# Six of twelve softmax tiles summed by accumulating transfers, four multiplied with the context in three rounded terms

## The chip, the cores and the metric

The kernel runs on one core of one Trainium2 chip. The metric is the device time of one execution in microseconds; the time of the kernel before is the median of three runs. The core has a matrix engine (TensorE, PE in the profile; its weight loads are PEld), a vector engine (VectorE, DVE), an activation engine (ScalarE, ACT), a general engine (GpSimd, POOL), a queue that only issues transfers (SyncE, SP) and 16 DMA engines. Each engine runs its own queue in order, and the queues meet in semaphores. Transfers issued by SP are on the queue that the profile calls q1, those issued by POOL on q0.

## The reference

One layer of cross attention and one of experts, in float32: 8 batches of 56 query tokens against 1500 context tokens, 16 heads of 64, width 128.

```
q, k, v = layernorm(x) @ Wq, ctx @ Wk, ctx @ Wv          # split into 16 heads
dots = q @ k.T / 8  - (1 - mask) * 1e6                   # the mask is of the query row
x = x + (softmax(dots) @ v) @ Wout + bout
h = gelu(layernorm(x) @ w1[e] + b1[e])                   # batch e goes to expert e
out = x + h @ w2[e] + b2[e]
```

## The kernel before, in words

The key weights are folded into the queries and the value weights into the output weights, so that both attention products are taken with the context itself. A batch is a product of scores (context by 16 x 56 = 896 query columns), an exponential, and a product of the exponentials with the context.

The context is cut into 12 **tiles** of 125 rows. A batch is 12 **steps** t = 0 to 11 (`iteration` on each engine). In step t, PE makes the scores of tile t (`scores`, L405): three terms of rounded operands, high times high, high times low, low times high, each in two halves of 448 columns. Such a rounded operand has the type F32R in the code. ACT takes the exponential (`exponentials`, L639) into a ring of six buffers, `ex`, and then copies the row of shifts into the PSUM buffer that the scores of tile t + 2 will be added to (`seed`, L644). PE multiplies the exponentials of tile t - 2 with the context (`probs_ctx`, L433), in plain float32, two halves of 448 columns, accumulating over all 12 tiles in `ps_a`. The products of tiles 10 and 11 fall into steps 0 and 1 of the next batch.

VectorE adds up the exponentials of the 12 tiles (`add_tile`, L807), 11 additions a batch, at places given by `ADD_AT`: tiles 1 and 2 in step 3, then 3, 4 and 5 in steps 5, 7 and 9, the others from step 10 on, and 10 and 11 at the start of the next batch. The sum over the rows is then a small PE product (`sum_jobs`), for which ACT rounds the sum (`sum_high_part`, L655) and VectorE takes the rest (`sum_low_part`, L952).

Beside this, each batch prepares the next one. In 21 max jobs PE makes the scores once more in one rounded term (`max_job`, L450), at the places in `MAX_AT`, and VectorE takes their maxima (`max_part`, L810). They share two PSUM banks, and a job waits until the job two before it has been drained. From the maxima VectorE makes the shifts (`shifts`, L815 to L821), behind the last max job; PE spreads them in step 10 (`shift_jobs`, L419). The last batch has no such jobs. Every second batch from batch 2 on also carries the expert layer of two batches.

POOL loads and rounds the next batch's context (`ctxt_hi_load`, L1104), and takes the low parts of its queries (L1096) and of its context (`ctxt_lo_chunk`, L1114) at steps 2, 3, 6 and 7. SP loads the raw context (`load_ctxt`, L283) once these low parts are made, and the context by rows (`load_ctx`, L289).

The wait that guards a buffer of the ring:

```
wait(act, pv_done, b.at(TM, t - RING + 1))
wait(act, ex_summed, ...)
nc.scalar.activation(half(ex[0:MT, slot, :]), src, ACT.Exp, scale=SCALE).then_inc(ex_ready, 1)
```

Of the kernel before, what the change touches and what calls it, by code (L numbers as in the profile page):

```python
# [32 lines left out]
ALU = mybir.AluOpType  # L33
# [67 lines left out]
def xattn_ffn(nc, x_pairs, ctx, ctx_t, mask_q, wq_t, wk_t, wv_t, w_out, b_out, w1, b1_t, w2, b2, out):  # L101
# [15 lines left out]
    RING = 6  # L117
    assert D == P and MT * TM == M and QT * P == Q and MC * KM == M and E == B and TM % RING == 0
# [23 lines left out]
    ADD_AT = {(3, 0): (1, 2), (5, 1): (3,), (7, 1): (4,), (9, 1): (5,), (10, 0): (6,), (10, 2): (7,), (11, 0): (8, 9)}  # L142
    ADD_LATE = (10, 11)
# [7 lines left out]
    with ExitStack() as stack:  # L151
# [16 lines left out]
        ex = sb("ex", [P, RING, Q])  # L168
# [12 lines left out]
        wqk_raw = ex[:, :, :].rearrange("p r q -> p (r q)")[:, 0:2 * HP * P].rearrange("p (w j d) -> p w j d", w=2, j=HP)  # L181
# [58 lines left out]
        last_half = sem("last_half")  # L240
        ex_summed, pv_done, att_ready = sem("ex_summed"), sem("pv_done"), sem("att_ready")
# [9 lines left out]
        block = stack.enter_context(nc.Block())  # L251

# [20 lines left out]
        def _(sp):  # L273
# [353 lines left out]
        def _(act):  # L627
# [3 lines left out]
            def exponentials(b, t):  # L631

                slot = t % RING
# [3 lines left out]
                wait(act, pv_done, b.at(TM, t - RING + 1))  # L637
                wait(act, ex_summed, b.at(TM - 1, max(t - RING, 1)) if t >= RING else b.at(TM - 1, t - RING + 1))
# [564 lines left out]
```

## Time and profile before

| | |
|---|---|
| median of 3 runs | 386.22 us (385.52 to 386.38) |
| the profiled execution's own time | 386.32 us |
| its span in the trace | 384.6 us |
| TensorE busy | 372.8 us, 97% |
| VectorE busy | 299.6 us, 78% |
| ScalarE busy | 222.6 us, 58% |
| GpSimd busy | 75.8 us, 20% |
| moved by DMA | 25.00 MB |

The span is the time between the first and the last instruction in the trace; the rest of the profiled execution's own time, 1.7 us, lies around it. A busy share is a mean over the whole span, and several engines can be busy at once.

### The profile page before, as it was taken

How to read it: one execution, taken by the hardware profiler on the slowest of the kernel's cores; microseconds unless marked ns; L12 is line 12 of the kernel's file. 1: busy time of each engine (PE TensorE's matmuls, PEld its weight loads, DVE VectorE, ACT ScalarE, POOL GpSimd, SP SyncE). 2: the span in 40 equal slices, each digit the busy share in tenths (PEclk: the TensorE clock that was granted, in tenths of full speed). 3: DMA queues.
4: the chain of work that ended last, by engine and by line, in shares of the span. 5: the costliest groups of instructions: out<-in, count | busy, mean ns of one | idle time of the engine just before them, and what ended most of it. 6: DMA issues, size and time to landing. Idle time of an engine off the chain costs nothing.

```text
span 384.6 us, 5442 instructions
## 1 busy us (share of the span) xinstructions
PE 372.8 (97%) x1661; PEld 268.2 (70%) x1661; DVE 299.6 (78%) x472; ACT 222.6 (58%) x294; POOL 75.8 (20%) x68
## 2 busy tenths in 40 slices
PE   6999999999999999999999999999999999999994
PEld 6767776677767876677767776777667876676663
DVE  4888677987798669987898679987898679466553
ACT  3556354785468346775577446775577355856521
POOL 0703300720073000810081001800090000000000
PEclk9999999999999999999999999999999999999999
DMA  7665020350035000334035000243032000300000
GB/s 246 220 184 145 2 80 1 82 147 13 3 81 142 20 1 1 87 101 167 0 84 153 3 0 18 84 131 123 0 96 64 0 0 2 115 0 2 0 3 5
DMA packets 23686, 25.00 MB, mean 65 GB/s; under 512 B 1240, under 2 KB 20600, under 8 KB 23672
## 3 DMA queue, kind: packets, MB, share of 16 engines
q1 hardware_dynamic: 20648, 19.45, 16.7%
q0 software_dynamic: 3024, 5.38, 5.4%
q8 instruction: 8, 0.13, 0.1%
q14 instruction: 6, 0.05, 0.1%
HBM read 24.59 MB, written 0.23 MB: 65 GB/s over the span
## 4 chain that ended last, share of the span: by engine, by line
PE 76%; DVE 13%; issue 7%; DMA 1%; ACT 1%; DVEq 1%; SPq 0%; ACTq 0%
PE ps_a L433 29%; PE ps_s L405 24%; PE ps_x L450 9%; PE ps_x L483 4%; DVE ex_sum L807 4%; DVE chunk_max L810 2%; PE ps_a L382 2%; PE ps_x L503 2%; PE ps_x L512 1%; DVE shift_diag L821 1%; DMA ex<-in_wk_t 1%; PE ps_x L465 1%; PE ps_x L466 1%; PE ps_x L419 1%; DVE hid L911 1%
## 5 line engine op out<-in xcount | busy, mean ns | idle before, releaser
L433 PE MATMUL ps_a<-ex,ctx_sb 125*128 125x448 f32 x376 | 167.9, 541 | 0.0
L810 DVE TENSOR_REDUCE chunk_max<-ps_x 128x1 f32<-128x500 f32 x168 | 110.9, 675 | 30.0 <-PE ps_x L450 26.8
L639 ACT ACTIVATE ex<-ps_s 125x896 f32<-125x896 f32 x96 | 88.0, 916 | 70.4 <-PE ps_s L405 68.9
L807 DVE TENSOR_TENSOR ex_sum<-ex_sum,ex 125x896 f32<-125x896 f32 x80 | 91.9, 1149 | 6.7 <-ACT ex L639 5.4
L644 ACT COPY ps_s<-shift_row 125x896 f32<-125x896 f32 x94 | 85.6, 911 | 16.8 <-DVE shift_row L947 14.3
L433 PEld LDWEIGHTS ps_a<-ex,ctx_sb 125*128 125x128 f32 x376 | 69.9, 190 | 25.7 <-issue 19.8
L405 PE MATMUL ps_s<-qk_hi,ctxt_hi 128*125 128x448 f32 x192 | 87.1, 535 | 0.0
L450 PE MATMUL ps_x<-ctxt_hi,qk_hi 128*128 128x500 f32 x168 | 84.0, 503 | 1.3 <-DVE chunk_max L810 0.9
L405 PEld LDWEIGHTS ps_s<-qk_hi,ctxt_hi 128*125 128x125 f32 x192 | 36.0, 187 | 35.1 <-issue 35.0
L405 PE MATMUL ps_s<-qk_hi,ctxt_lo 128*125 128x448 f32 x192 | 54.8, 367 | 0.0
L405 PE MATMUL ps_s<-qk_lo,ctxt_hi 128*125 128x448 f32 x192 | 54.6, 366 | 0.0
L1104 POOL DMA_DIRECT2D ctxt_hi<-in_ctx_t x21 | 11.7, 557 | 175.6 <-PE ps_s L405 173.6
L450 PEld LDWEIGHTS ps_x<-ctxt_hi,qk_hi 128*128 128x128 f32 x168 | 31.5, 188 | 18.2 <-DVE chunk_max L810 9.7
L1114 POOL TENSOR_TENSOR ctxt_lo<-ctxt_raw,ctxt_hi 128x500 fp32r<-128x500 f32 x24 | 40.2, 1688 | 9.3 <-DVE ctxt_hi L827 9.3
L405 PEld LDWEIGHTS ps_s<-qk_hi,ctxt_lo 128*125 128x125 f32 x192 | 35.5, 185 | 4.4
L405 PEld LDWEIGHTS ps_s<-qk_lo,ctxt_hi 128*125 128x125 f32 x192 | 35.6, 185 | 3.4
L1096 POOL TENSOR_TENSOR qk_lo<-qk,qk_hi 128x448 fp32r<-128x448 f32 x16 | 22.2, 1389 | 18.1 <-DVE qk_hi L831 17.2
L685 ACT ACTIVATE logv<-veps 128x1 f32<-128x1 f32 (+2 forms) x7 | 1.4, 204 | 24.9 <-DVE veps L893 22.7
L483 PEld LDWEIGHTS ps_x<-w_vo,att_n 128*128 128x128 f32 (+1 forms) x128 | 14.4, 178 | 1.7 <-DVE chunk_max L810 1.1
L838 DVE TENSOR_TENSOR log_sum<-ps_x,inv_sum 128x448 f32<-128x448 f32 x16 | 9.3, 619 | 7.7 <-ACT inv_sum L672 7.7
L483 PE MATMUL ps_x<-w_vo,att_n 128*128 128x128 f32 (+1 forms) x128 | 15.1, 276 | 0.0
L666 ACT ACTIVATE log_sum<-ps_x 128x448 f32<-128x448 f32 x16 | 7.9, 541 | 9.6 <-PE ps_x L466 6.9
(96 smaller groups left out, 264.0 us busy)
## 6 DMA issues: line engine op xcount, KB each, us to landing
ctxt_raw<-in_ctx_t SPq DMA_DIRECT2D x8, 750.0 KB, 7.3
ctx_sb<-in_ctx SPq DMA_DIRECT2D x8, 750.0 KB
ctxt_hi<-in_ctx_t POOLq DMA_DIRECT2D x21, 250.0 KB, 3.5
w_sb<-in_w SPq DMA_DIRECT2D x4, 512.0 KB, 3.8
w_sb<-in_w SPq DMA_DIRECT2D x8, 256.0 KB, 4.3
ex<-in_wq_t SPq DMA_DIRECT2D x2, 256.0 KB, 3.6
ex<-in_wk_t SPq DMA_DIRECT2D x2, 256.0 KB, 4.5
att_n<-in_wv_t SPq DMA_DIRECT2D x1, 512.0 KB, 6.0
```

Of the source, the lines that this page charges most:

```text
L405: mm = nc.tensor.matmul(dst[c], a[:, u, rows], q[:, u, chunks[c]], start=(n == 0 and not seed), stop=(n == 2 and seed), skip_group_check=seed)
L433: mm = nc.tensor.matmul(ps_a[:, c, 0:CH], ctx_sb[0:MT, u, t, :], ex[0:MT, t % RING, c * CH:(c + 1) * CH], start=(t == 0), stop=(t == TM - 1))
L450: nc.tensor.matmul(bank[:, 0:MC], qk_hi[:, u, t * P:(t + 1) * P], ctxt_hi[:, u, k * MC:(k + 1) * MC], start=True, stop=True).then_inc(job_ ...
L483: mm = nc.tensor.matmul(bank[pair.tokens(), 0:D], att_n[:, h, pair.tokens()], w_vo[:, h, :], start=(h == 0), stop=(h == HEADS - 1))
L639: nc.scalar.activation(half(ex[0:MT, slot, :]), src, ACT.Exp, scale=SCALE).then_inc(ex_ready, 1)
L644: nc.scalar.copy(ps_s[0:MT, t % 2, :, 0:CH], half(shift_row[0:MT, b.parity, :])).then_inc(seeded, 1)
L807: nc.vector.tensor_tensor(dst, left, ex[0:MT, t % RING, :], ALU.add).then_inc(ex_summed, 1)
L810: nc.vector.tensor_reduce(chunk_max[:, k, t:t + 1], filled()[:, 0:MC], AX.X, ALU.max).then_inc(job_free, 1)
L838: nc.vector.tensor_tensor(log_sum[:, cols], bank[:, 0:CH], inv_sum[:, cols], ALU.mult).then_inc(job_free, 1)
L1096: nc.gpsimd.tensor_tensor(qk_lo[:, b.parity, cols], b.pick(qk)[:, cols], qk_hi[:, b.parity, cols].bitcast(F32), ALU.subtract).then_inc(qk_ ...
L1104: pool.dma_start(ctxt_hi[:, b.parity, cols], ctx_t[bass.ds(b.at(1, 0), 1), :, cols].rearrange("a d m -> d (a m)")).then_inc(ctxt_hi_in[k], 16)
L1114: nc.gpsimd.tensor_tensor(ctxt_lo[:, b.parity, cols], ctxt_raw[:, cols], ctxt_hi[:, b.parity, cols].bitcast(F32), ALU.subtract).then_inc(c ...
```

## The change: what it does

The 11 additions of a batch on VectorE become 5, and 6 accumulating transfers. The buffers of tiles 0, 1 and 2 are three chains; when tile t (3 to 8) has its exponentials, POOL issues a transfer that adds its buffer onto chain t mod 3, once that chain's own product and its earlier transfer are done. VectorE then adds chain 1 and chain 2 to chain 0 and tiles 9, 10 and 11 to that. The ring behind the chains has four buffers, so the exponential of tile t (7 to 11) waits for the transfer (or the sum) of tile t - 4. The transfers take all 128 partitions, of which the last three are filled with zeros once at the start.

Tiles 2, 4, 6 and 8 are multiplied with the context in three rounded terms, as the scores are: ACT rounds the exponentials (`ex_high_part`), VectorE subtracts (`ex_low_part`), and PE makes six products in place of two. The order of the products is 0, 1, 3, 2, 5, 4, 7, 6, 9, 8, 10, 11, so a rounded tile comes one place later and the odd tile ahead of it one place earlier. The context of these four tiles is split once a batch, on ACT in step 7 and on POOL in step 10 of the batch before. The expert layer's hidden buffers move into an array that is free by then.

```diff
-    RING = 6
-    assert D == P and MT * TM == M and QT * P == Q and MC * KM == M and E == B and TM % RING == 0
+    CHAINS, RING, LAST_DMA = 3, 4, 8
+    SUMS = CHAINS - 1 + TM - 1 - LAST_DMA
+    SPLIT = [2, 4, 6, 8]
+    PV_ORDER = [0, 1, 3, 2, 5, 4, 7, 6, 9, 8, 10, 11]
+    SPLITS, CTX_HI_AT, CTX_LO_AT = len(SPLIT), 7, 10
...
-    ADD_AT = {(3, 0): (1, 2), (5, 1): (3,), (7, 1): (4,), (9, 1): (5,), (10, 0): (6,), (10, 2): (7,), (11, 0): (8, 9)}
-    ADD_LATE = (10, 11)
+    ADD_AT = {(10, 2): (0,), (11, 0): (1, 2)}
+    ADD_LATE = (3, 4)
+    LAST_ADD_AT = {(10, 2): (0,), (11, 0): (1, 2), (11, 1): (3,)}
...
-        ex = sb("ex", [P, RING, Q])
+        ex_all = sb("ex_all", [P, CHAINS + RING, Q])
+        ex_hi = sb("ex_hi", [P, 2, Q], F32R)
+        ex_lo = sb("ex_lo", [P, 2, Q], F32R)
+        ctx_hi = sb("ctx_hi", [P, 2, SPLITS, D], F32R)
+        ctx_lo = sb("ctx_lo", [P, 2, SPLITS, D], F32R)
...
+            sp.wait_ge(zeros_ready, 1)
+            sp.wait_ge(fold_drained, 4)
+            sp.dma_start(ex_all[MT:P, :, :], ex_sum[0:P - MT, 1, :].unsqueeze(1).to_broadcast([P - MT, CHAINS + RING, Q])).then_inc(rows_cleared, 16)
...
+            def probs_ctx(b, slot, between=None):
+                u, t = b.parity, PV_ORDER[slot]
...
+                if t in SPLIT:
+                    n = SPLIT.index(t)
+                    pe.wait_ge(ctx_lo_ready, b.at(1, 1))
+                    pe.wait_ge(ex_lo_ready, b.at(SPLITS, n + 1))
+                    for term, (a, e) in enumerate([(ctx_hi, ex_hi), (ctx_hi, ex_lo), (ctx_lo, ex_hi)]):
+                        if term == 2 and between is not None:
+                            between()
+                        for c in range(2):
+                            mm = nc.tensor.matmul(ps_a[:, c, 0:CH], a[0:MT, u, n, :], e[0:MT, n % 2, c * CH:(c + 1) * CH],
+                                                  start=False, stop=False)
+                    mm.then_inc(pv_done, 1)
+                    return
...
+                if t < CHAINS:
+                    wait(act, ex_summed, b.at(SUMS, max(t, 1) - SUMS))
+                elif t < CHAINS + RING:
+                    before = max(s for s in range(CHAINS, TM) if (s - t) % RING == 0)
+                    wait(act, pv_done, b.at(TM, read_by(before) - TM))
+                    if before > LAST_DMA:
+                        wait(act, ex_summed, b.at(SUMS, CHAINS - 1 + before - LAST_DMA - SUMS))
+                else:
+                    act.wait_ge(pv_done, b.at(TM, read_by(t - RING)))
+                    added_by_dma(act, b, t - RING)
+                nc.scalar.activation(half(ex(t)[0:MT, :]), src, ACT.Exp, scale=SCALE).then_inc(ex_ready, 1)
...
+            def ex_high_part(b, n):
+                t = SPLIT[n]
+                act.wait_ge(ex_ready, b.at(TM, t + 1))
+                if n >= 2:
+                    act.wait_ge(pv_done, b.at(TM, read_by(SPLIT[n - 2])))
+                nc.scalar.copy(ex_hi[0:MT, n % 2, :], ex(t)[0:MT, :]).then_inc(ex_hi_ready, 1)
+            def ctx_high_part(b):
+                act.wait_ge(ctx_in[b.parity], b.at_every_other(16, 16))
+                nc.scalar.copy(ctx_hi[0:MT, b.parity, :, :], ctx_split(b)).then_inc(ctx_hi_ready, 1)
...
+                    if t == CTX_HI_AT and prepare:
+                        ctx_high_part(b.later(1))
+                    if t in SPLIT:
+                        ex_high_part(b, SPLIT.index(t))
...
+            def add_to_sum(b, n):
                 dst = ex_sum[0:MT, b.parity, :]
-                left = ex[0:MT, 0, :] if t == 1 else dst
-                if t > 1:
-                    dve.wait_ge(ex_summed, b.at(TM - 1, t - 1))
-                nc.vector.tensor_tensor(dst, left, ex[0:MT, t % RING, :], ALU.add).then_inc(ex_summed, 1)
+                if n < CHAINS - 1:
+                    for j in range(n + 2):
+                        added_by_dma(dve, b, LAST_DMA - CHAINS + 1 + j)
+                    left, part = ex(0)[0:MT, :] if n == 0 else dst, ex(n + 1)[0:MT, :]
+                else:
+                    t = LAST_DMA + n - CHAINS + 2
+                    dve.wait_ge(ex_ready, b.at(TM, t + 1))
+                    left, part = dst, ex(t)[0:MT, :]
+                wait(dve, ex_summed, b.at(SUMS, n))
+                nc.vector.tensor_tensor(dst, left, part, ALU.add).then_inc(ex_summed, 1)
+            def ex_low_part(b, n):
+                dve.wait_ge(ex_hi_ready, b.at(SPLITS, n + 1))
+                wait(dve, pv_done, b.at(TM, read_by(SPLIT[n - 2]) if n >= 2 else read_by(SPLIT[n - 2]) - TM))
+                nc.vector.tensor_tensor(ex_lo[0:MT, n % 2, :], ex(SPLIT[n])[0:MT, :], ex_hi[0:MT, n % 2, :].bitcast(F32),
+                                        ALU.subtract).then_inc(ex_lo_ready, 1)
...
+                    for n in (ADD_AT if prepare else LAST_ADD_AT).get(at, ()):
+                        add_to_sum(b, n)
+                    if (at[0] - 1, at[1]) in [(t, 2) for t in SPLIT]:
+                        ex_low_part(b, SPLIT.index(at[0] - 1))
...
+            def add_by_dma(b, t):
+                pool.wait_ge(ex_ready, b.at(TM, t + 1))
+                if t < 2 * CHAINS:
+                    pool.wait_ge(pv_done, b.at(TM, read_by(t - CHAINS)))
+                else:
+                    added_by_dma(pool, b, t - CHAINS)
+                pool.sem_inc(add_may_go, 1)
+                pool.dma_start(ex(t % CHAINS), ex(t), accum_op=ALU.add).then_inc(ex_added[t % CHAINS], 16)
+            def ctx_low_part(b):
+                pool.wait_ge(ctx_hi_ready, b.at(1, 1))
+                nc.gpsimd.tensor_tensor(ctx_lo[0:MT, b.parity, :, :], ctx_split(b), ctx_hi[0:MT, b.parity, :, :].bitcast(F32),
+                                        ALU.subtract).then_inc(ctx_lo_ready, 1)
...
+                    if CHAINS < t <= LAST_DMA + 1:
+                        add_by_dma(b, t - 1)
+                    if prepare and t == CTX_LO_AT:
+                        ctx_low_part(b.later(1))
```

The end of the first batch on **VectorE**, from the max jobs of steps 7 and 8 to the last addition in that batch. Before:

```order
L810 TENSOR_REDUCE chunk_max<-ps_x 128x1 x5
L807 TENSOR_TENSOR ex_sum<-ex_sum,ex 125x896
L815 TENSOR_REDUCE row_max<-chunk_max 128x7
L817 SCALAR_TENSOR_TENSOR row_max<-row_max,negpen 128x7
L819 SCALAR_TENSOR_TENSOR row_max<-row_max,negpen 128x7
L821 TENSOR_TENSOR shift_diag<-ident,row_max 128x896
L807 TENSOR_TENSOR ex_sum<-ex_sum,ex 125x896
L947 COPY shift_row<-ps_x 128x448 x2
L807 TENSOR_TENSOR ex_sum<-ex_sum,ex 125x896 x3
```

And now, at the same place:

```order
L897 TENSOR_REDUCE chunk_max<-ps_x 128x1 x4
L893 TENSOR_TENSOR ex_lo<-ex_all,ex_hi 125x896
L902 TENSOR_REDUCE row_max<-chunk_max 128x7
L904 SCALAR_TENSOR_TENSOR row_max<-row_max,negpen 128x7
L906 SCALAR_TENSOR_TENSOR row_max<-row_max,negpen 128x7
L908 TENSOR_TENSOR shift_diag<-ident,row_max 128x896
L1034 COPY shift_row<-ps_x 128x448 x2
L887 TENSOR_TENSOR ex_sum<-ex_all 125x896
L887 TENSOR_TENSOR ex_sum<-ex_sum,ex_all 125x896 x2
```

Ahead of the shifts a subtraction (tile 8) stands where the addition of tile 5 stood, the addition between the shifts and the copies of their rows is gone, and three additions stay behind the copies.

**POOL** in the first batch, behind the load of the next batch's rounded context. Before (`att_n` is cleared once, in this batch alone):

```order
L1096 TENSOR_TENSOR qk_lo<-qk,qk_hi 128x448
L1114 TENSOR_TENSOR ctxt_lo<-ctxt_raw,ctxt_hi 128x500
L1096 TENSOR_TENSOR qk_lo<-qk,qk_hi 128x448
L1124 MEMSET att_n 128x2048
L1114 TENSOR_TENSOR ctxt_lo<-ctxt_raw,ctxt_hi 128x500 x2
```

And now, where the rows on `ex_all` are the accumulating transfers of tiles 3 to 8:

```order
L1182 TENSOR_TENSOR qk_lo<-qk,qk_hi 128x448
L1200 TENSOR_TENSOR ctxt_lo<-ctxt_raw,ctxt_hi 128x500
L1182 TENSOR_TENSOR qk_lo<-qk,qk_hi 128x448
L1210 DMA ex_all<-ex_all 128x896 x2
L1230 MEMSET att_n 128x2048
L1210 DMA ex_all<-ex_all 128x896
L1200 TENSOR_TENSOR ctxt_lo<-ctxt_raw,ctxt_hi 128x500
L1210 DMA ex_all<-ex_all 128x896
L1200 TENSOR_TENSOR ctxt_lo<-ctxt_raw,ctxt_hi 128x500
L1210 DMA ex_all<-ex_all 128x896 x2
L1214 TENSOR_TENSOR ctx_lo<-ctx_sb,ctx_hi 125x512
```

The second and third low part of the next batch's context now stand behind the transfers of tiles 5 and 6, which wait for those tiles' exponentials.

## Rows read from the trace of the kernel before

**Rows 1.** The page's totals: busy us (share of the span) and instructions of each engine.

```profile
span 384.6 us, 5442 instructions
PE 372.8 (97%) x1661; PEld 268.2 (70%) x1661; DVE 299.6 (78%) x472; ACT 222.6 (58%) x294; POOL 75.8 (20%) x68
```

**Rows 2.** Waits of PE: total us, times, longest.

```profile
PE ps_x L419 <- DVE shift_diag L821: 1.1, 3, 0.4
PE ps_x L450 <- DVE chunk_max L810: 0.9, 2, 0.7
```

**Rows 3.** Chain that ended last, inside batch 5: start us, us, what.

```profile
251.86 1.50 PE ps_a L433 x4
253.37 1.22 PE ps_s L405 x6
254.59 0.23 PE ps_x L450
```

**Rows 4.** Groups by line: busy us, mean ns of one; idle before, releasers.

```profile
L810 DVE TENSOR_REDUCE chunk_max<-ps_x 128x1 f32<-128x500 f32 x168 | 110.9, 675 | 30.0 <-PE ps_x L450 26.8
L639 ACT ACTIVATE ex<-ps_s 125x896 f32<-125x896 f32 x96 | 88.0, 916 | 70.4 <-PE ps_s L405 68.9 <-DVE ex_sum L807 0.8 <-PE ps_s L419 0.4
L1104 POOL DMA_DIRECT2D ctxt_hi<-in_ctx_t x21 | 11.7, 557 | 175.6 <-PE ps_s L405 173.6 <-issue 0.9
L1114 POOL TENSOR_TENSOR ctxt_lo<-ctxt_raw,ctxt_hi 128x500 fp32r<-128x500 f32 x24 | 40.2, 1688 | 9.3 <-DVE ctxt_hi L827 9.3
```

**Rows 5.** Tile ex_sum: duration in ns, shortest/median/longest; first and last start.

```profile
L807 DVE TENSOR_TENSOR ex_sum<-ex_sum,ex x80: 1071/1084/1928, 42.4 to 363.7; 125x896 f32<-125x896 f32 x80
L655 ACT CAST sum_hi<-ex_sum x7: 937/939/941, 74.2 to 328.5; 125x896 fp32r<-125x896 f32 x7
L952 DVE TENSOR_TENSOR sum_lo<-ex_sum,sum_hi x7: 1093/1379/1384, 75.9 to 329.5; 125x896 fp32r<-125x896 f32 x7
```

**Rows 6.** ACT in batch 5: exponentials of tiles 3, 7, 8, 11; next batch's start.

```profile
252.87 0.92 ACT L639 ACTIVATE ex<-ps_s 125x896 f32<-125x896 f32 x1
...
264.86 0.92 ACT L639 ACTIVATE ex<-ps_s 125x896 f32<-125x896 f32 x1 [1.48 <-PE ps_s L405]
...
268.34 0.92 ACT L639 ACTIVATE ex<-ps_s 125x896 f32<-125x896 f32 x1 [1.62 <-PE ps_s L405]
...
277.61 0.91 ACT L639 ACTIVATE ex<-ps_s 125x896 f32<-125x896 f32 x1
...
283.58 0.94 ACT L655 CAST sum_hi<-ex_sum 125x896 fp32r<-125x896 f32 x1 [1.40 <-DVE ex_sum L807]
```

**Rows 7.** Timeline, end of batch 6 (step 10).

```profile
318.88 1.09 DVE L821 TENSOR_TENSOR shift_diag<-ident,row_max 128x896 fp32r<-128x896 f32 x1
...
320.11 0.67 PE L419 MATMUL ps_x<-shift_diag,ones_r 128*128 128x448 f32 x2 [0.37 <-DVE shift_diag L821]
```

**Rows 8.** Timeline, end of the last batch (steps 10 and 11, then the sum).

```profile
360.01 0.43 DVE L929 TENSOR_TENSOR hid<-hid,hid_u 128x256 f32<-128x256 f32 x1 [0.65 <-ACT hid_u L700]
...
363.71 1.09 DVE L807 TENSOR_TENSOR ex_sum<-ex_sum,ex 125x896 f32<-125x896 f32 x1 [1.63 <-ACT ex L639]
...
364.43 1.02 PE L433 MATMUL ps_a<-ex,ctx_sb 125*128 125x448 f32 x2
...
365.28 1.67 PE L463 MATMUL ps_x<-ex_sum,ones 125*128 125x448 f32 x4
```

**Rows 9.** The page's transfers: queues (packets, MB, share), and issues (KB, us to landing).

```profile
q1 hardware_dynamic: 20648, 19.45, 16.7%
q0 software_dynamic: 3024, 5.38, 5.4%
...
ctxt_raw<-in_ctx_t SPq DMA_DIRECT2D x8, 750.0 KB, 7.3
...
ctxt_hi<-in_ctx_t POOLq DMA_DIRECT2D x21, 250.0 KB, 3.5
```

**Rows 10.** Transfers from 238 to 260 us, 40 slices of 0.55 us: GB/s.

```profile
GB/s 0 0 22 153 335 349 262 204 73 0 0 0 0 0 0 0 0 25 70 79 108 109 110 108 109 109 108 142 142 109 110 62 0 0 15 60 182 410 375 346
```

More of the change, by code:

```diff
@@ L251, in xattn_ffn, with ex, ctx_split, read_by @@
         block = stack.enter_context(nc.Block())
+        def ex(t):
+            return ex_all[:, t if t < CHAINS else CHAINS + (t - CHAINS) % RING, :]
+        def ctx_split(b):
+            return ctx_sb[0:MT, b.parity, :, :].rearrange("p (t r) d -> p r t d", r=2)[:, SPLIT[0] % 2, SPLIT[0] // 2:SPLIT[-1] // 2 + 1, :]
+        def read_by(t):
+            return PV_ORDER.index(t) + 1
+        def added_by_dma(eng, b, t):
+            adds = LAST_DMA // CHAINS
+            eng.wait_ge(ex_added[t % CHAINS], b.at(16 * adds, 16 * (t // CHAINS)))
         def half(t):
@@ L631, in exponentials @@
             def exponentials(b, t):
-                slot = t % RING
                 src = ps_s[0:MT, t % 2, :, 0:CH]
                 act.wait_ge(scores_ready, b.at(TM, t + 1))
-                wait(act, pv_done, b.at(TM, t - RING + 1))
-                wait(act, ex_summed, b.at(TM - 1, max(t - RING, 1)) if t >= RING else b.at(TM - 1, t - RING + 1))
-                nc.scalar.activation(half(ex[0:MT, slot, :]), src, ACT.Exp, scale=SCALE).then_inc(ex_ready, 1)
+                if b.i is None and b.off == 0 and t == 0:
+                    act.wait_ge(rows_cleared, 16)
+                if t < CHAINS:
[18 more added lines that the diff above has]
+                nc.scalar.copy(ctx_hi[0:MT, b.parity, :, :], ctx_split(b)).then_inc(ctx_hi_ready, 1)
             def seed(b, t):
@@ L729, in iteration @@
                         sum_high_part(b.later(-1))
+                    if t == 1 and first:
+                        ctx_high_part(b)
+                    if t == CTX_HI_AT and prepare:
+                        ctx_high_part(b.later(1))
+                    if t in SPLIT:
+                        ex_high_part(b, SPLIT.index(t))
                     if pair is not None and t == GELU_AT[0]:
@@ L996, in between @@
                     if not prepare and at == (TM - 1, 2):
[L997 removed]
+                        add_to_sum(b, SUMS - 1)
                 def add(at):
@@ L1001, in add @@
                         for n in ADD_LATE:
-                            add_tile(b.later(-1), n)
-                    if prepare:
-                        for n in ADD_AT.get(at, ()):
-                            add_tile(b, n)
-                    elif at[0] > 1 and at[1] == 0:
-                        add_tile(b, at[0] - 1)
+                            add_to_sum(b.later(-1), n)
+                    for n in (ADD_AT if prepare else LAST_ADD_AT).get(at, ()):
+                        add_to_sum(b, n)
+                    if (at[0] - 1, at[1]) in [(t, 2) for t in SPLIT]:
+                        ex_low_part(b, SPLIT.index(at[0] - 1))
                 for t in range(TM):
```

34 lines of the change are left out of this document (19 added, 15 removed).

## The prediction

> **What bounds the kernel now.** I read the page's totals first: TensorE is busy for 372.8 of 384.6 us, VectorE for 299.6, ScalarE for 222.6 [rows 1]. A share of 97% need not mean that nothing else decides, so I read what PE waits for: the last-ending wait behind the shifts costs 1.1 us in three waits, the one behind the maxima 0.9 us in two [rows 2]. These are the only waits inside the batches, where the other engines wait for PE instead: ScalarE sat idle 68.9 us for the scores, VectorE 26.8 us for the max jobs [rows 4]. So a batch is as long as PE's own work, and that is the place to price.
>
> The chain of batch 5 gives the prices [rows 3]. The scores of one tile are six products of rounded operands and take 1.22 us, 0.203 us each. The float32 product of one tile with the context is two instructions, four records, and takes 1.50 us. A max job takes 0.23 us. A full step with three max jobs is 1.22 + 1.50 + 3 x 0.23 = 3.41 us.
>
> **The change part by part.**
>
> *PE.* A rounded tile takes six products of 448 columns by 125 rows, the same shape and operand type as the scores, so 1.22 us in place of 1.50. That saves 0.28 us on 4 tiles in 8 batches: 32 x 0.28 = 9.0 us. Everything else is whether something takes this back.
>
> *VectorE.* Six additions of 1.08 us a batch go, four subtractions come. The nearest row for one is the low part of the sum, same size and types: 1.09 us at best, 1.38 us in the median [rows 5]. Per batch that is 6 x 1.08 - 4 x 1.09 = 2.1 us less work at the lower bound, 1.0 us less at the upper. The engine has room; the order matters more. Ahead of the shifts the subtraction of tile 8 stands where the addition of tile 5, 1.08 us, stood, so the shifts are made no earlier. In batch 6 PE already waits 0.37 us for them there [rows 7]. Between the last max job and the shift jobs lies one rounded product (tile 6), so PE now comes 0.28 us earlier to the same end: the wait becomes 0.65 us. That takes 0.28 us back in batches 2, 4 and 6 (0.84 us), and about 0.2 us in batch 0; in the odd batches the last max job is a place earlier, and the saving is kept. Behind the shifts one addition less lets the copies of the shift rows, and the additions behind them, start earlier; I give 0.5 us of the 0.9 us wait at the maxima back for that.
>
> *Where GpSimd now works beside VectorE.* The 1.38 against 1.09 us is a subtraction beside GpSimd's work at the start of a batch against one in the last batch, where GpSimd has none [rows 5]; an addition went up to 1.93 us. The second low part of the next batch's context (1.69 us, [rows 4]) used to run early in the batch; it now stands behind the transfer of tile 5, in steps 5 and 6, where tile 4's subtraction is. I take 0.15 us of PE's wait for a drained bank in seven batches, 1.0 us; the bounds are nothing and 0.85 us each (1.93 - 1.08), 6 us in all. The Trainium skill (SBUF — State Buffer, "Who interferes with whom") says that a VectorE instruction with two SBUF inputs contends with a GpSimd instruction that reads SBUF; the trace agrees by the two durations above, and by the page alone each such meeting could cost what the rows show.
>
> *ScalarE.* Four roundings of 0.94 us (the row of `sum_hi`, [rows 5]) and one of the context, 512 columns, under 0.94 us. In steps 7 and 8 ScalarE sat idle for 1.48 and 1.62 us before the exponential [rows 6], so 0.94 us in every second step fits; behind tile 2's rounding stand the logarithms, which wait for PE anyway. Cost: nothing. Without that cover it would be 0.94 us on the chain from scores to seed.
>
> *The new order of products.* Tile 3 is wanted one place earlier: its exponential ends at 252.87 + 0.92 = 253.79 us [rows 6], and the product in its new place would begin at 254.81, behind the max job at 254.59 [rows 3]. No wait.
>
> *The end.* In the last batch VectorE had one addition left at the end; now it has five, from the end of step 10. It is free there after 360.01 + 0.43 us [rows 8]. PE being 0.56 us ahead by then, it starts at 359.9 and ends five additions of 1.09 later at 365.3; the addition before ended at 364.8. PE would have been ready at 365.45 before, and now 1.12 us earlier, at 364.3: it waits 1.0 us. The last batch gains next to nothing.
>
> *The accumulating transfers.* Six a batch, each 128 x 896 x 4 = 459 KB. Issuing costs POOL 0.56 us each [rows 4], and POOL has the time. The trace shows no accumulating transfer, so I bound w, the time one keeps the DMA engines. Queue q0 moved 5.38 MB in 5.4% of 384.6 us, 259 GB/s [rows 9]; in slices of the load of `ctxt_hi` alone 349 GB/s, and 410 at best [rows 10]. Lower bound: one pass at 410, 1.1 us. Upper bound: reading the source, reading the target and writing, one behind the other at 259, 5.3 us. I take two passes at 349, 2.6 us, since rows of 3584 B are longer than the loads' rows and reads and writes can overlap. The Trainium skill (Collectives: The Full Stack, "The bandwidth ceiling") says that an add in the DMA path costs no cycles, but reads two sources through the same ring and so halves the rate. No run here shows that; by it the transfer would take twice a copy, also 2.6 us as an estimate, and by a copy's single pass 1.3.
>
> What w may be: in an odd batch tile 3's exponential ends at 253.79 us, and the rounding of the whole sum, ahead of the next batch's second exponential, begins at 283.58 [rows 6]: 29.8 us. Off that go the issue (0.56), the landing (3.5 us for 256 KB less 1.0 us at 259 GB/s, 2.5), four additions behind tile 8's transfer (4.4) and the raw context load, which moves from early in the batch into this stretch because it waits for the low parts behind the transfers (768 KB at 19.45 MB in 16.7% of 384.6 us, 303 GB/s: 2.5). 19.8 us stay for six: w up to 3.3 us is free. From tile 8 alone: its exponential ends at 269.26, and its chain is wanted by the second addition behind the copies of the shift rows, about when tile 11's exponential begins at 277.61 [rows 6], so 8.3 us from one to the other. With w = 2.6 the landing takes 0.56 + 2.5 + 2.6 = 5.7 us.
>
> **The sum.** 9.0 - 0.84 - 0.2 - 1.0 (GpSimd) - 1.0 (the end) + 0.5 = 6.5 us. The profiled execution's own time is 386.3 us (span 384.6), 0.1 above the median. 386.3 - 6.5 = **379.8 us**.
>
> **The rivals.**
>
> *A, the forecast*, 377.3 (all of the 9.0 us) to 382.
>
> *B, VectorE takes back more.* Subtractions at 1.93 us beside GpSimd, or transfers that land up to 1 us late: 5 us more lost, 382 to 385.4. For it: the longest addition, and two PSUM banks only. Against it: 30 us idle on VectorE, in every step.
>
> *C, no change.* The two above together eat the 6.5 us: 385.5 to 387.
>
> *D, the transfers become the bound; slower.* If w is above 3.3 us, the last of six lands late; sums, the next batch's exponentials behind `sum_high_part`, and PE wait 6 x (w - 3.3) us. In batches 2, 4 and 6 the expert layer's products stretch the steps and leave more room, so five batches count. At w = 4.0 that is 4.2 us in five, 21 us: 386.3 - 6.5 + 21 = 401. At 5.3 it is 12 us, 60 us: 440. It decides from w = 3.5, where five batches lose the 6.5 us. For it: q0's mean rate in two passes gives w = 3.5 already [rows 9]; against it: full slices move 349 to 410 GB/s [rows 10].
>
> **How the numbers follow.** A has 0.53, B 0.12, C 0.05, D 0.30. About 0.2% (0.8 us) is what a measurement of this kernel can tell from no change. Faster 0.65, same 0.05, slower 0.30. The range from 376.8 to 396 holds A, B, C and the part of D with w up to about 3.8; A's own is 377.3 to 382.
>
> **What would show it.** Right: the rounded products at 1.22 us a tile in the chain; PE's waits for `shift_diag` grown to some 0.6 us in even batches and one of 1 us for `ex_sum` at the end; no waits of ScalarE or VectorE for the accumulating transfers, which land in under 8 us. Wrong: those landings at 9 us or more, VectorE idle ahead of its first addition in step 10, ScalarE idle ahead of the exponentials of tiles 7 to 11 or of the next batch. Then the step on w failed. Subtractions of 1.3 us and more with PE waiting for maxima in steps 5 and 6 would mean B.

## The result and the profile after

The changed kernel takes 395.58 us (median of 4 runs, 394.01 to 396.91); the kernel before took 386.0 us beside it (385.52 to 386.38). The ratio is 1.0235, 95% interval 1.0194 to 1.0276: slower by 2.3%, where 1.7% faster was forecast. The profiled execution spans 395.0 us, 10.4 us more than before.

The page's totals, which answer to [rows 1]:

```profile
span 395.0 us, 5783 instructions
PE 374.2 (95%) x1725; PEld 284.6 (72%) x1725; DVE 289.9 (73%) x456; ACT 254.8 (65%) x334; POOL 126.5 (32%) x125
```

PE is busy for 1.4 us more than before, although its products should have become cheaper by 9.0 us, and stands still for 9.0 us more (395.0 - 374.2 against 384.6 - 372.8): it waits more, and it works slower somewhere. What PE waits for, against [rows 2] (total us, times, longest):

```profile
PE ps_x L497 <- DVE chunk_max L897: 8.6, 8, 1.9
PE ps_x L454 <- DVE shift_diag L908: 2.2, 5, 0.6
...
PE ps_x L510 <- DVE ex_sum L887: 1.4, 1, 1.4
```

The wait for maxima has grown from 0.9 to 8.6 us. The next question is where in a batch it sits. The starts of ScalarE's exponentials in the timeline cut a run into batches and steps; the table is worked out from them (a step from one exponential's start to the next, batch 6 for the single steps; end: from the last batch's twelfth exponential to the end of the span). The later rows belong to experiments below.

| us | batches 2, 4, 6 | batches 3, 5 | step 6 | step 8 | step 10 | end |
|---|---|---|---|---|---|---|
| before | 46.47, 46.56, 46.39 | 38.68, 38.65 | 3.33 | 4.96 | 4.39 | 21.84 |
| after | 50.57, 50.64, 50.57 | 38.09, 38.09 | 6.70 | 5.55 | 3.91 | 22.81 |
| tile 4's low part moved | 47.02, 47.45, 46.91 | 38.17, 38.16 | 3.40 | 5.55 | 3.92 | 22.8 |
| transfers alone | 45.52, 45.54, 45.45 | 38.75, 38.74 | 3.41 | 4.96 | 3.05 | 22.5 |
| and GpSimd's part moved | 46.02, 46.32, 46.03 | 38.13, 38.15 | 3.40 | 4.97 | 3.74 | 22.8 |
| three moves | 46.04, 46.17, 46.02 | 38.13, 38.14 | 3.41 | 4.96 | 3.75 | 21.6 |
| three moves, two tiles | 45.02, 44.99, 44.97 | 38.18, 38.19 | 3.41 | 4.96 | 2.86 | 21.6 |

The odd batches became 0.6 us shorter, the even ones 4.1 to 4.2 us longer. Most of that is one step, step 6 (3.4 us), then step 8 (0.6); step 10 is 0.5 us shorter, and step 11 gives that back. The timeline of the changed kernel there, batch 6:

```profile
309.49 0.86 POOL L1210 DMA_DIRECT2D ex_all<-ex_all  x1 [7.19 <-PE ps_a L473]
309.57 0.39 PE L497 MATMUL ps_x<-ctxt_hi,qk_hi 128*128 128x500 f32 x1
...
309.89 0.14 DVE L981 TENSOR_SCALAR half_veps<-meanvar 128x1 f32<-128x1 f32 x1
...
310.05 1.57 POOL L1200 TENSOR_TENSOR ctxt_lo<-ctxt_raw,ctxt_hi 128x500 fp32r<-128x500 f32 x1
310.20 0.39 PE L497 MATMUL ps_x<-ctxt_hi,qk_hi 128*128 128x500 f32 x1
...
310.23 2.35 DVE L893 TENSOR_TENSOR ex_lo<-ex_all,ex_hi 125x896 fp32r<-125x896 f32 x1 [0.19 <-DVE half_veps L981]
...
312.50 1.25 DVE L897 TENSOR_REDUCE chunk_max<-ps_x 128x1 f32<-128x500 f32 x2
312.67 1.55 POOL L1200 TENSOR_TENSOR ctxt_lo<-ctxt_raw,ctxt_hi 128x500 fp32r<-128x500 f32 x1
...
313.22 0.49 PE L497 MATMUL ps_x<-ctxt_hi,qk_hi 128*128 128x500 f32 x1 [1.88 <-DVE chunk_max L897]
```

Read it from the bottom. PE stands for 1.88 us, because its third max job needs a bank. The two banks were filled by the jobs at 309.57 and 310.20, and VectorE does not get to them before 312.50: ahead of them in its queue stand the expert layer's residual (the last of its six instructions is the row at 309.89) and then tile 4's subtraction, which takes 2.35 us. Its neighbours say why: POOL's subtraction runs from 310.05 to 311.62, beside 1.39 us of it, and the instruction is 1.27 us longer than the 1.08 us it takes alone. What PE does behind the wait, in windows of 2 us (the window's length, then busy us of PE, PEld, DVE, ACT and POOL with their instructions, granted clock, DMA share, GB/s):

```profile
308.00:310.00 2.00, 2.00 (x14) 1.85 (x12) 1.14 (x6) 0.00 (x0) 0.51 (x1) 1.00 0.00 0
310.00:312.00 2.00, 1.34 (x5) 0.57 (x3) 1.81 (x2) 1.90 (x4) 1.62 (x2) 1.00 0.60 115
312.00:314.00 2.00, 0.78 (x4) 0.56 (x4) 2.00 (x4) 1.21 (x2) 1.94 (x2) 1.00 0.94 172
314.00:316.00 2.00, 2.00 (x7) 1.62 (x6) 1.34 (x4) 0.00 (x0) 0.22 (x1) 0.60 0.93 172
316.00:318.00 2.00, 2.00 (x7) 1.68 (x7) 1.17 (x2) 0.82 (x1) 0.00 (x0) 0.54 0.00 0
318.00:320.00 2.00, 2.00 (x12) 1.79 (x11) 1.43 (x4) 1.56 (x3) 0.88 (x1) 1.00 0.00 0
```

From 314 to 318 us PE is granted 0.60 and 0.54 of its clock on average, which is the level of 1.2 GHz for most of that time, and gets through 7 products per window instead of 12 to 14. It is the same in batches 2 and 4. In the other batches tile 4's subtraction overlaps with POOL's by 0.2 us at most and takes 1.08 us. So in the even ones the late subtraction costs the batch twice, by the wait and by the clock behind it.

The other rows that the forecast named look as it said: the rounded product, in the chain that ended last, takes 1.23 us for its six products, against 1.50 in [rows 3]:

```profile
278.02 1.23 PE ps_a L473 x6
```

The page's queue q0 (packets, MB, share) and issues of transfers (KB, median us to landing), against [rows 9], and the groups of the new instructions (busy us, mean ns of one):

```profile
q0 software_dynamic: 9936, 27.40, 35.5%
...
ex_all<-ex_all POOLq DMA_DIRECT2D x48, 448.0 KB, 4.5
```

```profile
L1210 POOL DMA_DIRECT2D ex_all<-ex_all x48 | 42.2, 879 | 164.0 <-ACT ex_all L695 121.6 <-PE ps_a L473 38.3 <-issue 3.2
L893 DVE TENSOR_TENSOR ex_lo<-ex_all,ex_hi 125x896 fp32r<-125x896 f32 x32 | 38.5, 1203 | 1.9 <-DVE inv_sum L932 1.3 <-DVE half_veps L981 0.6
```

The transfers land in 4.5 us and nothing waits for them. The queue's share less that of before is 140.2 - 20.8 = 119 us for 48 transfers, so one keeps the DMA engines for about 2.5 us (an estimate from the two shares); the forecast took w = 2.6. An issue keeps POOL for 0.88 us, 0.32 more than assumed. The subtractions take 1.20 us on average, which looks harmless: 29 of 32 take about 1.09, and three take 2.35.

### The profile page after: what moved, and what is told of

Same layout as the page of the kernel before. It is cut to its first block, busy times and chain, and to the rows that moved or that the text cites. A ratio compares the mean times of both kernels' runs of the same rounds, so it can differ in the third digit from the quotient of the medians.

```text
span 395.0 us, 5783 instructions
## 1 busy us (share of the span) xinstructions
PE 374.2 (95%) x1725; PEld 284.6 (72%) x1725; DVE 289.9 (73%) x456; ACT 254.8 (65%) x334; POOL 126.5 (32%) x125
## 4 chain that ended last, share of the span: by engine, by line
PE 76%; DVE 14%; issue 6%; ACT 2%; DVEq 1%; ACTq 0%
PE ps_s L440 25%; PE ps_a L480 20%; PE ps_x L497 9%; PE ps_a L473 7%; PE ps_x L530 4%; DVE chunk_max L897 3%; DVE ex_sum L887 2%; PE ps_a L417 2%; PE ps_x L550 2%; DVE shift_diag L908 2%; DVE w_qk L1001 1%; PE ps_x L454 1%; PE ps_s L611 1%; PE ps_x L559 1%; PE ps_x L512 1%
## 5 line engine op out<-in xcount | busy, mean ns | idle before, releaser
L695 ACT ACTIVATE ex_all<-ps_s 125x896 f32<-125x896 f32 x96 | 88.0, 917 | 53.2 <-PE ps_s L440 51.9
L480 PE MATMUL ps_a<-ex_all,ctx_sb 125*128 125x448 f32 x248 | 110.6, 540 | 0.0
L1210 POOL DMA_DIRECT2D ex_all<-ex_all x48 | 42.2, 879 | 164.0 <-ACT ex_all L695 121.6
L497 PE MATMUL ps_x<-ctxt_hi,qk_hi 128*128 128x500 f32 x168 | 80.8, 484 | 8.9 <-DVE chunk_max L897 8.6
L440 PE MATMUL ps_s<-qk_hi,ctxt_hi 128*125 128x448 f32 x192 | 77.2, 483 | 0.0
L480 PEld LDWEIGHTS ps_a<-ex_all,ctx_sb 125*128 125x128 f32 x248 | 46.5, 189 | 16.5 <-issue 11.9
L887 DVE TENSOR_TENSOR ex_sum<-ex_sum,ex_all 125x896 f32<-125x896 f32 x32 | 39.9, 1246 | 1.4
L893 DVE TENSOR_TENSOR ex_lo<-ex_all,ex_hi 125x896 fp32r<-125x896 f32 x32 | 38.5, 1203 | 1.9 <-DVE inv_sum L932 1.3
L703 ACT CAST ex_hi<-ex_all 125x896 fp32r<-125x896 f32 x32 | 30.0, 937 | 0.0
L473 PE MATMUL ps_a<-ex_hi,ctx_lo 125*128 125x448 f32 x64 | 19.4, 384 | 0.0
```

What stands on the lines that cost most here:

```text
L440: mm = nc.tensor.matmul(dst[c], a[:, u, rows], q[:, u, chunks[c]], start=(n == 0 and not seed), stop=(n == 2 and seed), skip_group_check=seed)
L473: mm = nc.tensor.matmul(ps_a[:, c, 0:CH], a[0:MT, u, n, :], e[0:MT, n % 2, c * CH:(c + 1) * CH], start=False, stop=False)
L497: nc.tensor.matmul(bank[:, 0:MC], qk_hi[:, u, t * P:(t + 1) * P], ctxt_hi[:, u, k * MC:(k + 1) * MC], start=True, stop=True).then_inc(job_ ...
L695: nc.scalar.activation(half(ex(t)[0:MT, :]), src, ACT.Exp, scale=SCALE).then_inc(ex_ready, 1)
L703: nc.scalar.copy(ex_hi[0:MT, n % 2, :], ex(t)[0:MT, :]).then_inc(ex_hi_ready, 1)
L887: nc.vector.tensor_tensor(dst, left, part, ALU.add).then_inc(ex_summed, 1)
```

## Experiments

Each is an edit of the changed kernel. The first four ran on one chip beside the kernel before (386.23 us, median of 19 runs), the next four too (386.17, 27 runs), and the last three (386.31, 17 runs).

**Tile 4's low part ahead of the residual.**

```
+    EX_LO_AT = {2: (3, 2), 4: (5, 1), 6: (7, 2), 8: (9, 2)}
...
-                    if (at[0] - 1, at[1]) in [(t, 2) for t in SPLIT]:
-                        ex_low_part(b, SPLIT.index(at[0] - 1))
+                    for n, t in enumerate(SPLIT):
+                        if at == EX_LO_AT[t]:
+                            ex_low_part(b, n)
```

> The only edit: VectorE makes the low part of tile 4 one place earlier in a step, ahead of the residual of the expert layer instead of behind it; GpSimd's order is untouched. Theory 1 (order): in batches 2, 4 and 6 the subtraction of 2.35 us stands in front of two maxima whose banks are both full, PE waits 1.88 us for them and then works at the lower clock, about 1.6 us more; ahead of the residual VectorE was idle for 3.4 us, so all of it goes: 3 x 3.5 = 10.4 us less, about 385 us, no wait of PE for chunk_max over 0.8 us, and step 6 of those batches back to 3.4 us from 6.7. Theory 2 (the late transfer and GpSimd's work hold PE up wherever the subtraction stands): 391 us or more, and the wait of 1.9 us stays.

387.29 us, ratio to before 1.0025 (0.9992 to 1.0057): 8.3 us less than the changed kernel, and step 6 is back at 3.40 us. The timeline of this run, batch 6:

```profile
297.43 1.08 DVE L894 TENSOR_TENSOR ex_lo<-ex_all,ex_hi 125x896 fp32r<-125x896 f32 x1
...
302.94 1.58 POOL L1202 TENSOR_TENSOR ctxt_lo<-ctxt_raw,ctxt_hi 128x500 fp32r<-128x500 f32 x1
303.05 1.26 DVE L898 TENSOR_REDUCE chunk_max<-ps_x 128x1 f32<-128x500 f32 x2
...
303.78 0.67 PE L498 MATMUL ps_x<-ctxt_hi,qk_hi 128*128 128x500 f32 x1
```

The subtraction now runs while PE makes the residual's product, in 1.08 us, and the third max job finds its bank free. POOL's subtraction still runs at the same place; beside it now stand two maxima, with one operand that lies in PSUM, and they take what they always take (1.26 us for two, 675 ns each in [rows 4]). Theory 1 holds, though the median is 2 us above its 385.

**GpSimd's context parts in steps 4 and 5.** This takes the other half of the suspicion away: VectorE's order stays, the neighbour goes.

```
-    CTXT_LO_AT, QK_LO_AT = [2, 6, 7], [2, 3]
+    CTXT_LO_AT, QK_LO_AT = [2, 4, 5], [2, 3]
```

> The only edit: GpSimd makes the second and third low parts of the next batch's context in steps 4 and 5 instead of 6 and 7, away from the subtraction of tile 4, whose place on VectorE is untouched. Theory 1 (the length that contention adds is what counts): the subtraction goes from 2.35 to 1.08 us, PE's wait from 1.88 to 0.6 us, and such a wait does not lower the clock: 3 x 2.9 = 8.7 us less, 387 us. Theory 2 (the order alone counts, and any wait there lowers the clock): only 3 x 1.27 = 3.8 us less, 392 us. Theory 3 (no contention: the subtraction is long for another reason): unchanged, 395.6 us.

416.09 us, ratio 1.0766 (1.0704 to 1.0827): far off every theory. Two places of its timeline tell why, batch 5 and batch 6:

```profile
275.76 4.75 DVE L893 TENSOR_TENSOR ex_lo<-ex_all,ex_hi 125x896 fp32r<-125x896 f32 x1 [0.22 <-DVE inv_sum L932]
...
275.84 1.57 POOL L1200 TENSOR_TENSOR ctxt_lo<-ctxt_raw,ctxt_hi 128x500 fp32r<-128x500 f32 x1
...
277.66 1.90 POOL L1200 TENSOR_TENSOR ctxt_lo<-ctxt_raw,ctxt_hi 128x500 fp32r<-128x500 f32 x1
...
281.15 0.50 PE L497 MATMUL ps_x<-ctxt_hi,qk_hi 128*128 128x500 f32 x1 [3.08 <-DVE chunk_max L897]
...
332.25 1.09 DVE L893 TENSOR_TENSOR ex_lo<-ex_all,ex_hi 125x896 fp32r<-125x896 f32 x1 [0.19 <-DVE half_veps L981]
...
333.98 0.50 PE L497 MATMUL ps_x<-ctxt_hi,qk_hi 128*128 128x500 f32 x1 [0.63 <-DVE chunk_max L897]
```

At tile 4, where the edit aimed, the numbers are those of theory 1: 1.09 us, a wait of 0.63 us, the clock at 1.00 behind it, and step 6 falls from 6.70 to 4.31 us. The kernel before had 3.33 there: the 1.0 us that stays is what the place in the queue costs without the neighbour. But the two context parts now stand beside tile 2's subtraction, in batches 1 to 6. It takes 4.72 to 4.75 us: 1.08 and the 1.57 + 1.90 us of the two subtractions beside it make 4.55. So the place was badly chosen, the time of the whole says nothing about tile 4, and the size of the contention is shown twice: here too the instruction stands still for about as long as GpSimd subtracts.

**The transfers alone.** All twelve tiles as float32 products; no rounding, no subtraction, the order of products kept.

```
-                if t in SPLIT:
+                if t in []:
...
-                    if t in SPLIT:
-                        ex_high_part(b, SPLIT.index(t))
...
-                    if (at[0] - 1, at[1]) in [(t, 2) for t in SPLIT]:
-                        ex_low_part(b, SPLIT.index(at[0] - 1))
...
-                    if prepare and t == CTX_LO_AT:
-                        ctx_low_part(b.later(1))
```

> The accumulating transfers and the new order of products alone: all twelve tiles are float32 products, no rounding, no subtractions. Theory 1 (the transfers are free inside the batches, and the loss hangs on the subtractions): the 386.0 us of before plus about 1 us for the five additions at the end, 386 to 388 us, PE waiting for chunk_max 1 us or less in all. Theory 2 (transfers that land beside everything else, or GpSimd's later order, slow the batches by themselves): 390 us or more.

384.99 us, ratio 0.9958 (0.9927 to 0.9989): a little faster than the kernel before, and 1 us under the lower end of theory 1. The landing is 4.8 us here. The table shows where the gain is: the even batches are about 1.0 us shorter, the odd ones are not. In batch 6 step 10 takes 3.05 us instead of 4.39, since VectorE has no addition left ahead of the shifts; step 11 gives 0.7 us of that back, and step 0 is 0.3 us shorter. So it is not the transfers that cost.

**The wait filled.** TensorE gets products to do where it would stand still.

```
                     if c == 1 and between is not None:
+                        for _ in range(fill):
+                            nc.tensor.matmul(ps_a[:, 0, CH:CH + 64], ones[:, :], ones[:, 0:64], start=True, stop=True, ...)
                         between()
```

> The only edit: in step 6 of batches 2, 4 and 6 TensorE gets 16 products of 64 columns (about 1.7 us in all, their result is not used) just ahead of the max job for which it waits 1.88 us. Theory 1 (the granted clock falls because TensorE stands still there): the clock stays at its full level behind that place, and the 1.6 us that the products behind it lost come back three times, 4.8 us less, about 391 us. Theory 2 (the clock falls for another reason, or what follows waits for something else anyway): 395.6 us, unchanged, or a little more.

396.46 us, ratio 1.0265 (1.0203 to 1.0328). The filling was twice too long, 3.49 us for the 16 products, so what it won it also cost. (These products start a sum of their own in the bank in which the tiles' products are summed, and part of that sum is dropped; the run is read for its time alone.) With 8 products that only add into columns that nothing reads:

> As the run with 16 filling products, with 8 of them (1.75 us by that run's 3.49 us for 16), so that they fill the wait and add nothing to it; they add into columns that nothing reads. Theory 1 (the standstill is what lowers the clock): no slice below full clock behind it, step 6 of batches 2, 4 and 6 goes from 6.7 to about 5.2 us, 3 x 1.5 = 4.5 us less than the changed kernel, 391 us. Theory 2 (the slow stretch behind it has another cause): step 6 stays at 6.7 us and the time at 395.6 us.

392.78 us, ratio 1.0166 (1.0119 to 1.0213), 2.8 us less than the changed kernel by the medians and 4.8 by the spans; step 6 takes 5.54 to 5.56 us, and step 7 3.17 to 3.18, where the changed kernel had 3.51 to 3.61. The windows over the filled wait and behind it:

```profile
307.00:309.00 2.00, 2.00 (x15) 1.59 (x14) 2.00 (x1) 1.95 (x4) 1.57 (x3) 1.00 0.77 145
309.00:311.00 2.00, 1.85 (x11) 1.30 (x11) 1.97 (x5) 0.86 (x1) 1.88 (x2) 1.00 0.93 172
311.00:313.00 2.00, 2.00 (x11) 1.80 (x10) 1.82 (x5) 0.31 (x1) 0.00 (x0) 1.00 0.77 142
```

The max job starts as late as before, but the clock stays at 1.00. So of the 3.4 us that step 6 lost, about 1.2 come from the clock and the rest from the wait itself; the clock costs 0.4 us more in step 7, some 1.5 us a batch in all.

**GpSimd's part for the tiles moved away from the hidden values.** On top of tile 4's move:

```
-    SPLITS, CTX_HI_AT, CTX_LO_AT = len(SPLIT), 7, 10
+    SPLITS, CTX_HI_AT, CTX_LO_AT = len(SPLIT), 6, 7
```

and the call of `ctx_low_part` stands behind `ctxt_lo_chunk` in its step.

> Tile 4's low part ahead of the residual, as before, and in addition the rounding of the next batch's tiles moved to step 6 and GpSimd's subtraction for them to the end of step 7, away from the expert layer's hidden values. Theory 1 (a VectorE instruction with two SBUF operands stands still for as long as GpSimd subtracts beside it): the first of the two products of the hidden values (1.69 us, 0.69 in the kernel before) falls to 0.69 us, PE's wait of 0.7 us for chunk_max in step 8 or 9 goes, and step 8 from 5.54 to about 5.0 us: 3 x 0.6 = 1.7 us less than with tile 4's move alone, about 385.6 us. Theory 2 (the hidden values are slow because they now share one buffer with the weights): 1.69 us stays, no change.

383.87 us, ratio 0.9921 (0.9894 to 0.9948): faster than the kernel before. The instruction in question, in the timeline of the changed kernel with POOL's row beside it, and then in this run:

```profile
322.81 1.60 POOL L1214 TENSOR_TENSOR ctx_lo<-ctx_sb,ctx_hi 125x512 fp32r<-125x512 f32 x1
...
323.29 1.69 DVE L1001 SCALAR_TENSOR_TENSOR w_qk<-w_qk 128x512 f32<-128x512 f32 x1
```

```profile
312.62 0.69 DVE L1002 SCALAR_TENSOR_TENSOR w_qk<-w_qk 128x512 f32<-128x512 f32 x1
```

1.12 us beside POOL's subtraction had made it 1.00 us longer; step 8 falls from 5.55 to 4.97 us. The shared buffer has no part in it. This collision was in the change and in none of the forecast's terms.

In all these meetings but the one of 4.75 us GpSimd had begun first. The kernel's own additions show what happens otherwise; the start of batch 5 in the changed kernel:

```profile
247.64 3.03 DVE L887 TENSOR_TENSOR ex_sum<-ex_sum,ex_all 125x896 f32<-125x896 f32 x2
...
247.92 1.80 POOL L1182 TENSOR_TENSOR qk_lo<-qk,qk_hi 128x448 fp32r<-128x448 f32 x1 [0.67 <-DVE qk_hi L918]
...
251.75 1.14 POOL L1182 TENSOR_TENSOR qk_lo<-qk,qk_hi 128x448 fp32r<-128x448 f32 x1
```

The first of the two additions begins 0.28 us ahead of POOL's subtraction and is not longer than alone (the second begins 1.12 us behind it, at 248.76 us); POOL's subtraction takes 0.66 us more than the next one like it. The second addition begins while that subtraction still has 0.96 us to go, and takes 1.91 us, 0.83 more than alone. In these rows the instruction that begins later pays. The subtraction of 4.75 us is an exception: it began 0.08 us ahead of POOL's first and paid for both; why is not shown.

**Tile 8's low part behind the copies of the shift rows.** On top of tile 4's move: `8: (10, 2)` in `EX_LO_AT`, ahead of the additions there.

> Tile 4's low part ahead of the residual, and tile 8's low part behind the copies of the shift rows instead of ahead of the shifts. Theory 1 (1.08 us ahead of the shifts holds PE up at the shift jobs and ScalarE at the seeds): PE's waits for shift_diag fall from 2.2 us in five to under 0.5 us in all, step 10 from 3.9 to about 3.1 us in batches 2, 4 and 6 and by 0.3 us in the others: about 3 us less than with tile 4's move alone, 384 us. Theory 2 (PE then waits for tile 8's low part in step 11 instead): no gain, step 11 longer by 0.5 to 1 us.

389.22 us, ratio 1.0078 (1.0049 to 1.0108): slower than with tile 4's move alone. PE's waits in this run:

```profile
PE ps_x L498 <- DVE chunk_max L898: 5.7, 8, 0.8
PE ps_x L511 <- DVE ex_sum L888: 2.4, 1, 2.4
```

No wait at the shift jobs is left, as theory 1 said, and step 10 falls to 3.07 us. But in the even batches step 11 and step 0 of the next batch grow by 0.3 and 0.6 us, and PE waits 2.2 us more for maxima: 1.08 us put behind the shifts delays the additions, and the even batches end up as long as before the move. The loss is at the end of the program, 25.2 us against 22.8: there tile 8's low part stands directly ahead of the five additions, PE waits 1.0 us longer for `ex_sum` (2.42 us), and in the windows of 2 us behind that wait its clock is 0.85, 0.50 and 0.80, where it stays at 1.00 with tile 4's move alone (a wait of 1.41 us). Neither theory had the place right.

**All four moves at once**, with the last batch's additions spread over steps 10 and 11:

```
-    LAST_ADD_AT = {(10, 2): (0,), (11, 0): (1, 2), (11, 1): (3,)}
+    LAST_ADD_AT = {(10, 0): (0,), (10, 1): (1,), (10, 2): (2,), (11, 0): (3,)}
```

> All of it together: tile 4's low part ahead of the residual, tile 8's behind the copies of the shift rows, GpSimd's subtraction for the tiles in step 7, and in the last batch the first four additions spread over steps 10 and 11 as soon as their operands are there. If the causes found are all there is: 387.3 less 1.7 (hidden values), 3 (shifts) and 1.4 us (PE's wait for ex_sum at the end), about 381 us, faster than both kernels. If the moves only shift the waits on VectorE about: 385 us or more.

384.63 us, ratio 0.9957 (0.993 to 0.9984): between the two theories. Without tile 8's move:

> Tile 4's low part ahead of the residual, GpSimd's subtraction for the tiles in step 7, and in the last batch the first four additions spread over steps 10 and 11; tile 8's low part stays ahead of the shifts. Theory 1 (the five additions pushed together at the end cost what PE waits there): the wait of 1.4 us for ex_sum goes, 383.9 less 1.4 us, 382.5 us. Theory 2 (the last addition sets the end anyway, as in the kernel before): 383.5 us or more.

382.37 us, ratio 0.9902 (0.9875 to 0.993). The stretch at the end falls from 22.8 to 21.6 us; PE's wait for `ex_sum` there is 0.19 us. Theory 1, by the trace; the medians alone could not tell 1.5 us from the spread of the runs.

**Two tiles instead of four.** Even with three moves, batches 3 and 5 gain 0.5 us on the kernel before, where four tiles should bring 1.12. So not every tile pays:

```
-    SPLIT = [2, 4, 6, 8]
+    SPLIT = [4, 6]
```

> The same three moves, with only tiles 4 and 6 in three rounded terms; tiles 2 and 8 are float32 products again. Theory 1 (what tiles 2 and 8 save on TensorE, 0.28 us each, VectorE takes back, since their low parts stand in steps 3 and 9 where it has no room: in steps 4 to 5 and at the shifts): as fast as with four tiles or faster, 380 to 382.5 us. Theory 2 (each split tile gives its 0.28 us): 16 x 0.28 = 4.5 us slower than with four, 387 us.

379.67 us, ratio 0.9837 (0.9805 to 0.9869), the fastest kernel of this study and theory 1, a little below its 380. And its control, the transfers alone with the end spread:

> The accumulating transfers alone, no tile in three terms, with the additions at the end spread as well. Theory 1 (PE's wait of 0.9 us for ex_sum goes, nothing else moves): 385.0 less 0.9, 384.1 us. As the control of the run with two tiles: if two split tiles pay 0.28 us each in eight batches, that one is 4.5 us faster than this; if not, the two are within 1 us.

384.28 us, ratio 0.9946 (0.992 to 0.9971). Two tiles in three terms bring 4.6 us over none (about 0.5 to 0.6 in every batch): 16 x 0.28 = 4.5, so they bring all that they save. Four bring 1.9 us, and 32 x 0.28 would be 9.0. What PE waits for inside the batches with two tiles:

```profile
PE ps_x L498 <- DVE chunk_max L898: 0.9, 1, 0.9
...
PE ps_s L455 <- DVE shift_diag L909: 0.2, 1, 0.2
```

With four tiles batches 3 and 5 are no longer and no shorter than with two; in batch 6 step 10 is 0.89 us and the step of the residual 0.2 us shorter with two. Which of tiles 2 and 8 costs how much was not tried one by one; the two places point to tile 8 for most of it.

## Why the prediction was wrong

- **What bounds the kernel**: right. PE's own work sets a batch, and the 0.28 us per rounded tile are there: 1.23 against 1.50 us in the chain, and 4.6 us for 16 tiles where nothing stands against them.
- **Where GpSimd now works beside VectorE: this step failed.** It had the meeting right (the second context part moves behind tile 5's transfer and stands beside tile 4's subtraction), and took 0.15 us in seven batches, 1.0 us in all. Measured were 3.4 us in step 6 of each of three batches. Three things were wrong in it. Its price came from the longest addition of before, 0.85 us more than alone [rows 5], though the row of POOL's subtraction, 1.69 us [rows 4], was beside it. That addition began when the GpSimd subtraction beside it had 0.98 us to go, and lost most of that; tile 4's begins 0.18 us behind one of 1.57 us. The runs show that a VectorE instruction that begins second stands still for nearly the whole overlap (1.27 us for 1.39, 1.00 for 1.12). It looked at the length and not at the queue: in the even batches the subtraction stands behind the residual and ahead of two full banks, where the kernel before had no addition. And it did not ask what a standstill of PE does to the granted clock, 1.2 us of the 3.4 and 0.4 more in step 7. Moving the one instruction ahead of the residual takes back 8.3 of the 9.6 us (10.8 in the spans).
- **The same neighbour a second time**: POOL's new subtraction for the tiles against the hidden values, 0.6 us in step 8 of three batches and some more behind it (1.0 us a batch in all), was in no term. Its move brought 3.4 us in the medians.
- **The shifts**: a wait of 0.65 us in the even batches was forecast, and 0.6 us is the longest. What it does to ScalarE's seeds was left out: with tile 8 a float32 product, and tile 2 as well, ScalarE waits 8.2 us for the shift rows instead of 12.2, and step 10 is 0.89 us shorter in the even batches. That the odd batches keep their saving was wrong by half: 38.67 to 38.09 us, 0.6 of 1.12, and that is what two tiles bring there.
- **ScalarE** at nothing and **the order of products** without a wait: right. ScalarE still waits for scores, and with two or four tiles rounded no wait on it appears.
- **The end**: 1.0 us was forecast, a wait of 1.42 us and 0.97 us of length came.
- **The accumulating transfers**: right. They land in 4.5 us (5.7 had been worked out), keep the DMA engines for about 2.5 us each (w = 2.6) and cost nothing inside a batch; rival D, on which the whole chance of a slower kernel stood, did not happen. The kernel was slower by the mechanism of rival B, whose sign (long subtractions, PE waiting for maxima in steps 5 and 6) is what the trace shows, at three times its price. That 395.58 us still lies inside the range of 376.8 to 396 is luck: the range went so high for D alone.

The stretch ahead of the first exponential differs by up to 2.5 us from run to run, so the sum is taken from there to the end of the span: 352.6 us before, 362.7 after. Taken away one after the other, tile 4's subtraction is 10.3 us of that, the hidden values 3.0, the end 1.3 and tiles 2 and 8 together 3.2: that leads to the 344.9 us of the run with two tiles. The forecast stands for 352.6 - 6.5 = 346.1 us.

## What to carry to other kernels

When an instruction is added to an engine that is not the bottleneck, look at the queue at that place and not at its idle share: who stands behind it, how many buffers are full there, and when the bottleneck comes for one. Price a meeting of VectorE and GpSimd by who begins first, the later one standing still for what is left of the earlier, and look for every VectorE instruction with two operands in SBUF that the other engine's new order brings beside it. And try each part of a saving for itself: here two of the four rounded tiles earned the whole gain of the rounding, and the other two cost more than they saved.

## What the runs showed of the hardware

- A VectorE subtraction of 125 x 896 elements from two SBUF operands takes 1.08 us alone, 2.35 beside one GpSimd subtraction that began 0.18 us earlier and 4.75 beside two; an addition of the same size that began 0.28 us ahead of GpSimd's subtraction kept its length, and GpSimd's took 1.80 us instead of 1.14; two maxima of PSUM data beside such a subtraction take 1.25 us, no more than elsewhere. The Trainium skill (SBUF — State Buffer, "Who interferes with whom") calls the shared port an exclusive lock; the durations agree with that, and not with a slowdown in part.
- Behind a standstill of 1.88 us TensorE was granted 1.2 GHz for some 3.4 us (the windows above: 0.60 and 0.54 on average over two times 2 us, which 3.4 us at half the clock and the rest at the full clock would give), in three batches of three; with the wait filled by 8 products it kept 2.4 GHz. Behind waits of 0.63 and 1.41 us it kept 2.4 GHz too, behind one of 2.42 us it fell. The length of the wait alone doesn't tell: in the run with the context parts in steps 4 and 5 there were six standstills of 3.05 to 3.08 us; behind four of them the clock fell to 0.50, and behind those in batches 4 and 5 it stayed at 1.00. What tells them apart was not found.
- An accumulating transfer of 448 KB from SBUF to SBUF landed 4.5 to 4.8 us after its issue (median of 48), and its issue kept GpSimd's queue for 0.88 us, against 0.56 us for the loads of [rows 4]. No engine waited for the sums.
